# Making the first batch's key and query pieces inside the layer norm, and spreading the expert weight loads over the attention groups

## The reference

```python
x = x + _layernorm(attention(_layernorm(x)))
x = x + _layernorm(moe(_layernorm(x)))

# attention: 16 heads of 16, one key and one value head shared by all
latent = x @ Wc_down                       # 256 -> 128
q = (latent @ Wq_up).reshape(B, T, 16, 16)
k, v = split(latent @ Wkv_up)              # 16 + 16
att = softmax(where(causal, q @ k.T * 0.25, -inf))
y = (att @ v).reshape(B, T, 256) @ Wc_proj

# moe: each token goes to the expert with the largest logit (8 experts, hidden 1024)
y = disp + relu(LN(disp) * g + b @ W1 + b1) @ W2 + b2
```

## Time and profile before

| | us |
|---|---|
| median of 3 runs | 1006.48 |
| profiled execution | 1002.18 |
| its span, first to last instruction | 1000.2 |
| last copy of the latent ends (end of the layer norm) | 38.25 |
| first maxima matmul starts | 54.82 |
| first scores matmul starts | 78.08 |
| busy: PE / PEld / DVE / ACT / POOL | 862.1 / 527.6 / 698.1 / 535.9 / 300.6 |
| mean granted TensorE clock, share of full speed | 0.927 |

### The profile page before, as it was taken

One profiled execution on the slowest core, in us unless ns is written; L12 is line 12 of the kernel. 1 busy time (PEld: TensorE's weight loads), 2 busy tenths in 40 slices (PEclk: granted clock), 3 DMA queues, 4 the chain that ended last, 5 costly groups with the idle time before them and its releaser, 6 DMA issues. The chain is left out here.

```text
span 1000.2 us, 20703 instructions
## 1 busy us (share of the span) xinstructions
PE 862.1 (86%) x5630; PEld 527.6 (53%) x5631; DVE 698.1 (70%) x2447; ACT 535.9 (54%) x909; POOL 300.6 (30%) x565
## 2 busy tenths in 40 slices
PE   5768999999999999999999658851999999999994
PEld 3322333333333333333333147741999999999993
DVE  7457789888888888888886047866466666666652
ACT  3502666666666665666667523311566565656561
POOL 1201223332233322333322123313134344343311
PEclk9955999999999999999999977955999999999998
DMA  9330011111111111211000157732011001011000
GB/s 338 117 103 9 9 52 53 53 42 33 52 64 42 47 35 45 67 45 51 24 25 18 39 200 221 223 127 74 15 31 34 31 31 35 25 33 32 17 16 7
DMA packets 54739, 62.88 MB, mean 63 GB/s; under 512 B 12526, under 2 KB 45958, under 8 KB 54544
## 3 DMA queue, kind: packets, MB, share of 16 engines
q1 hardware_dynamic: 50928, 53.67, 16.1%
q0 software_dynamic: 3744, 8.40, 2.6%
HBM read 35.86 MB, written 9.55 MB: 45 GB/s over the span
## 5 line engine op out<-in xcount | busy, mean ns | idle before, releaser
L592 ACT ACTIVATE PR<-ST 128x1024 f32<-128x1024 f32 (+1 forms) x256 | 239.0, 969 | 150.0 <-PE ST L516 148.4
L645 DVE CUSTOM_DVE_ANT_0 junk<-ring,causal 128x384 bf16<-128x384 f32 (+3 forms) x512 | 220.4, 485 | 35.2 <-PE ring L485 35.0
L485 PE MATMUL ring<-K,Q 96*128 96x512 bf16 (+3 forms) x768 | 208.7, 342 | 41.1 <-DVE MP L645 11.1
L648 DVE TENSOR_REDUCE MP<-ring 128x1 f32<-128x512 f32 x256 | 163.2, 680 | 44.5 <-PE ring L485 44.4
L516 PE MATMUL ST<-Q,K 99*128 99x512 bf16 (+3 forms) x768 | 179.6, 330 | 10.3 <-DMA Q<-MT 6.9
L759 POOL TENSOR_SCALAR_AFFINE_SELECT PR<-PR 128x512 f32<-128x512 f32 x96 | 60.9, 634 | 303.1 <-ACT PR L592 297.8
L1436 PEld LDWEIGHTS hp<-XNT,WS 128*128 128x128 f32 x1248 | 147.8, 195 | 4.9 <-DVE XNT L1508 3.0
L1436 PE MATMUL hp<-XNT,WS 128*128 128x128 f32 x1248 | 148.4, 278 | 2.3 <-DVE XNT L1508 2.3
L485 PEld LDWEIGHTS ring<-K,Q 96*128 96x128 bf16 x768 | 65.8, 99 | 158.2 <-DVE MP L645 59.6
L1444 PE MATMUL yp<-W2s,HT 128*128 x624 | 141.2, 379 | 0.7 <-DVE z L1520 0.7
L533 PE MATMUL OB<-PR,V 128*32 128x512 f32 (+2 forms) x1152 | 124.3, 534 | 0.2
(11 more groups left out here) (173 smaller groups left out, 903.0 us busy)
## 6 DMA issues: line engine op xcount, KB each, us to landing
Q<-T SPq DMA_DIRECT2D x192, 64.0 KB, 2.6
W1s<-in_L_ffn_W_dram SPq DMA_DIRECT2D x8, 1024.0 KB, 12.1
W2s<-in_L_ffn_W_dram SPq DMA_DIRECT2D x8, 1024.0 KB, 7.3
Y<-in_L_attn_x_dram SPq DMA_DIRECT2D x8, 512.0 KB, 6.7
Y<-W1s SPq DMA_DIRECT2D x32, 128.0 KB
XQ<-in_L_attn_x_dram SPq DMA_DIRECT2D x8, 512.0 KB, 3.8
x_rows<-XQ SPq DMA_DIRECT2D x8, 512.0 KB, 7.3
W1s<-den_rows SPq DMA_DIRECT2D x15, 256.0 KB
```

Source lines behind the costliest of these rows:

```text
L485: last = pe.matmul(bank[:, at:at + w], Q[0:NR, g, i // BW, h, i % BW * P:(i % BW + 1) * P], K[b % 2][0:NR, k * NQ:k * NQ + w], start=True, ...
L592: act.activation(PR[t % RB][:, heads[0]:heads[-1] + 1, off:NQ], unit_of(ST[(NU * n + u) % 2], s), ACT.Exp, scale=SCALE).then_inc(exp_done, 1)
L645: op = dve.tensor_tensor_reduce(junk[:, done % 2, at:at + w], src, causal[:, NQ - w:NQ], 1.0, LOWEST, ALU.add, ALU.max, dst)
L648: op = dve.tensor_reduce(dst, src, AX, ALU.max)
```

## The change

It does these things.

1. The six pieces of the first batch move into the layer norm block, in the order k0, q00, k1, q01, q10, q11, at steps 2, 2, 3, 3, 4 and 5 (`FIRST_AT`). At each of these steps TensorE makes the pieces behind the transposes of the step and the `down` of the step before; ScalarE copies part 1 and part 2 at the end of its step; VectorE subtracts at the end of its step, behind the inverse; GpSimd makes part 3 one step later. Two PSUM banks (`room`) and two remainders (`left`) are used in turn.
2. SP sends the first batch's keys and the queries of groups 0 and 1 (6 and 24 DMAs) inside the layer norm block; the queries of groups 2 and 3 are sent at steps s = 5 and s = 9 of group n = 0, 12 DMAs each, without waits.
3. The six W1 loads leave the layer norm block; one is issued at s = 4 of each of the groups n = 0 to 5.
4. Of the four tiles of a layer norm step, VectorE normalises two and GpSimd two. GpSimd's WqT and its constants for K come after its tiles of step 0, the other constants after those of step 1.
5. The copy of the transposes is one instruction of 1024 columns in place of two of 512. The `alone` increments go from the block.

```diff
-FIRST = ("k0", "k1", "q00", "q01", "q10", "q11")
+FIRST = ("k0", "q00", "k1", "q01", "q10", "q11")
+FIRST_AT = {2: ("k0", "q00"), 3: ("k1", "q01"), 4: ("q10",), 5: ("q11",)}
...
             @block.sync
...
-                for e in range(LATE):
-                    sp.dma_start(W1s[:, :, e * F:(e + 1) * F], w1_v[e]).then_inc(w1_in, 16)
+
+                def made(name, part):
+                    sp.wait_ge((first1, first2, first3)[part], FIRST.index(name) + 1)
+
+                sp.wait_ge(ones_set, 6)
+                send_keys(sp, 0, made)
+                for g in range(2):
+                    send_queries(sp, g, made)
...
             @block.gpsimd
...
+                def third(name):
+                    i, _, rest = spot(name)
+                    pool.wait_ge(first2, i + 1)
+                    pool.tensor_tensor(parts(name)[2], rest, parts(name)[1], ALU.subtract).then_inc(first3, 1)
+
+                for t in range(N1):
+                    pool.wait_ge(rstd, t + 1)
+                    past(pool, xt_ready, t - 1)
+                    for i in range(HT, QT):
+                        normalise(pool, t, i).then_inc(xn_pool, 1)
...
+                    for name in FIRST_AT.get(t - 1, ()):
+                        third(name)
...
             @block.vector
...
+                def remainder(name):
+                    i, bank, rest = spot(name)
+                    dve.wait_ge(first1, i + 1)
+                    past(dve, first3, i - 1)
+                    dve.tensor_tensor(rest, bank, parts(name)[0], ALU.subtract).then_inc(first_left, 1)
...
+                for t in range(N1):
+                    if t + 1 < N1:
+                        statistics(t + 1, (t + 1) % 2)
+                    dve.wait_ge(rstd, t + 1)
+                    past(dve, xt_ready, t - 1)
+                    for i in range(HT):
+                        normalise(dve, t, i).then_inc(xn_dve, 1)
+                    if t + 1 < N1:
+                        inverse(t + 1, (t + 1) % 2)
+                    for name in FIRST_AT.get(t, ()):
+                        remainder(name)
...
             @block.tensor
...
+                for t in range(N1):
                     for i in range(QT):
-                        pe.wait_ge(xn_ready, QT * t + i + 1)
+                        if i < HT:
+                            pe.wait_ge(xn_dve, HT * t + i + 1)
+                        else:
+                            pe.wait_ge(xn_pool, HT * t + i - HT + 1)
...
                     last.then_inc(xt_ready, 1)
-                    if beyond(t, 0):
-                        down(t - 1, 1 - k)
-
-                passes(pe, step)
-                down(N1 - 1, 1)
+                    if t:
+                        down(t - 1, (t - 1) % 2)
+                    for name in FIRST_AT.get(t, ()):
+                        i, bank, _ = spot(name)
+                        if i == 0:
+                            pe.wait_ge(wq_turned, 1)
+                        pe.wait_ge(lt_copied, int(name[-1]) + 1)
+                        past(pe, first_left, i - 1)
+                        piece(pe, 0, name, bank).then_inc(first_ready, 1)
+                down(N1 - 1, (N1 - 1) % 2)
...
             @block.scalar
...
+                for t in range(N1):
+                    if t + 1 < N1:
+                        root(t + 1, (t + 1) % 2)
+                    act.wait_ge(xt_ready, t + 1)
+                    act.activation(XT[t % 2][:, :, :], xtp[t % 2][:, :, :], ACT.Copy).then_inc(xt_copied, 1)
+                    if t:
+                        latent(t - 1, (t - 1) % 2)
+                    for name in FIRST_AT.get(t, ()):
+                        i, bank, _ = spot(name)
+                        act.wait_ge(first_ready, i + 1)
+                        act.activation(parts(name)[0], bank, ACT.Copy).then_inc(first1, 1)
+                    for name in FIRST_AT.get(t, ()):
+                        second(name)
+                latent(N1 - 1, (N1 - 1) % 2)
...
         @block.tensor
...
-            pe.wait_ge(masks_made, 6)
-            pe.wait_ge(wq_turned, 1)
-            for name in FIRST:
-                piece(0, name, first_room(name)[0]).then_inc(first_ready, 1)
-            pe.wait_ge(resid, len(FIRST))
             for k in range(EVENT_AT[0]):
                 event(k)
...
         @block.sync
...
-            send_keys(0)
-            for g in range(NG):
-                send_queries(0, g)
             sends(0, EVENT_AT[0])
             for n in range(NB):
                 b, g = divmod(n, NG)
                 for s in range(len(STEPS)):
+                    if n == 0 and s in (5, 9):
+                        send_queries(sp, 2 if s == 5 else 3, lambda name, part: None)
+                    if s == 4 and n < LATE:
+                        sp.dma_start(W1s[:, :, n * F:(n + 1) * F], w1_v[n]).then_inc(w1_in, 16)
```

More of the change, by code:

```diff
@@ L96, in piece_no, with rows_of @@
 def piece_no(b, name):
-    return b * len(FIRST) + (ORDER if b else FIRST).index(name)
+    return (b - 1) * len(ORDER) + ORDER.index(name)
+def rows_of(name):
+    return HD if name[0] == "k" else P
 LEAD = 38
@@ L224, in attention, with parts, weights, piece @@
         eps_set = sem("eps_set")
+        k_in = sem("k_in")
+        q_in = [sem(f"q_in{g}") for g in range(NG)]
+        def parts(name):
+            c = int(name[-1])
+            if name[0] == "k":
+                return [t[:, c * NQ:(c + 1) * NQ] for t in (K1, K2, K3)]
+            return [t[:, int(name[1]), c * NQ:(c + 1) * NQ] for t in (T1, T2, T3)]
+        def weights(name):
+            if name[0] == "k":
+                return Wkv[:, 0:HD]
+            half = 2 * int(name[1])
+            return WqT[:, half:half + 2, :, :].rearrange("p g d h -> p (g d h)")
+        def piece(pe, b, name, bank):
+            c = int(name[-1])
+            return pe.matmul(bank, weights(name), LT[:, b * T + c * NQ:b * T + (c + 1) * NQ], start=True, stop=True)
+        def send_keys(sp, b, made):
+            for r, part in sorted(enumerate(KPART), key=lambda row: row[1]):
+                made("k1", part)
+                sp.dma_start(K[b % 2][r * HD:(r + 1) * HD, :], (K1, K2, K3)[part][:, :]).then_inc(k_in, 16)
+        def send_queries(sp, g, made):
+            half, quarter = divmod(g, 2)
+            rows = slice(quarter * GH * HD, (quarter + 1) * GH * HD)
+            for r, part in enumerate(QPART):
+                made(f"q{half}1", part)
+                for c in range(QC):
+                    sp.dma_start(Q[r * HD:(r + 1) * HD, g, c, :, :].rearrange("d h q -> d (h q)"),
+                                 (T1, T2, T3)[part][rows, half, c * NQ:(c + 1) * NQ]).then_inc(q_in[g], 16)
         with ExitStack() as c2:
@@ L374, in latent, with second @@
                     act.wait_ge(lt_ready, t + 1)
[L375 to L385, removed]
-                root(0, 0)
-                passes(act, step)
-                latent(N1 - 1, 1)
+                    act.activation(LT[:, t * (QT * P):(t + 1) * (QT * P)], ltp[k][:, :], ACT.Copy).then_inc(lt_copied, 1)
+                def second(name):
+                    i, _, rest = spot(name)
+                    act.wait_ge(first_left, i + 1)
+                    act.activation(parts(name)[1], rest, ACT.Copy).then_inc(first2, 1)
+                root(0, 0)
+                for t in range(N1):
[12 more added lines that the diff above has]
+                latent(N1 - 1, (N1 - 1) % 2)
         PR = [sb(f"PR{k}", [P, GH, NQ]) for k in range(RB - 1)]
@@ L456, in _ @@
         def _(pe):
[L457 to L465, removed]
             def values(b, bank):
@@ L501, in event @@
                 else:
[L502 removed]
+                    last = piece(pe, a, b, bank[0:rows_of(b), :])
                 last.then_inc(ring_ready, 1)
@@ L602, in _, with first_part @@
         def _(dve):
[L603 to L608, removed]
+            def first_part(k, b, name):
                 parts_sent(dve, b, name)
@@ L773, in _, with made @@
         def _(sp):
[L774 to L786, removed]
-                    made(b, f"q{half}1", part)
-                    for c in range(QC):
-                        sp.dma_start(Q[r * HD:(r + 1) * HD, g, c, :, :].rearrange("d h q -> d (h q)"),
-                                     (T1, T2, T3)[part][rows, half, c * NQ:(c + 1) * NQ]).then_inc(q_in[g], 16)
+            def made(b):
+                return lambda name, part: sp.wait_ge((part1, part2, part3)[part], piece_no(b, name) + 1)
             def send_max(r, c):
```

116 lines of the change are left out of this document (42 added, 74 removed).

## The result

The changed kernel takes 1008.59 us (median of 12 runs, 1005.82 to 1013.29), the kernel before in the same session 1005.24 (12 runs, 1001.14 to 1007.67). The ratio is 1.0042, 95% interval 1.0029 to 1.0056: slower by 4.2 us, 2.9 to 5.6 (the two medians lie 3.4 us apart; the ratio is made from all runs). The forecast was +3.5 with 0.58 on slower. The profiled execution takes 1005.82 in place of 1002.18, its span is 1004.1 in place of 1000.2. It is the fastest of the 12 runs of the changed kernel. In it the first scores come 3.6 us later, so nearly all of the difference is there by then.

A forecast was written before the change was run, and what follows sets the result against it. Two waits on SP's issue-bound queue stood at the head of the attention. -16.1 - 6.9 + 18.5 (longer layer norm) + 8.0 (clock) = +3.5 us, so 1006.5 becomes 1010.0 us; range 1001.5 to 1014.0.

The forecast's parts named there:

- 0.58 on slower: Whole kernel: the chance given to the change making it slower, against 0.22 for faster and 0.20 for same.
- maxima one hand-over behind the layer norm: Head of the attention: pieces and first sends leave it, so the maxima start right behind the layer norm, -16.1 us.
- scores no longer wait for SP: First scores: with SP's list empty the m row goes out when MT is written, so scores follow the events, -6.9 us.
- steps 0 and 1: Start of the layer norm: these steps don't move much, transposes of step 2 at about 16.7 in both kernels, 0 us.
- loop, at full clock, from step 2 to the end: Layer norm: engine orders close a loop at steps 2 to 5, 8.45 us a two-piece cycle; layer norm ends 18.5 us later.
- clock: Layer norm: four idle gaps of 3.85 us each lose TensorE's full clock, +8 us, with 0 and 24 as the ends.
- first scores: Attention: first scores start at 81.6 in place of 78.08, the sum of all terms, +3.5 us.
- The 2 us a gap: Layer norm gaps: assumed cost of returning to full clock, nearer to the kernel start's 1.5 us lost; +8 for four gaps.
- GpSimd's tile at 0.6 us: Layer norm: GpSimd's normalisation put between a copy (0.411) and a two-input operation (0.772), so 1.2 us a step.
- The first rival: Layer norm: the clock holds through the 3.85 us gaps, sum -4.5, 1002.0 us; chance 0.2.
- the smaller edits: GpSimd's two tiles 0; single 1024-column copy worth nothing; W1 loads hidden by a lead; deferred query DMAs fit into holes.
- the term it called "added": Layer norm: it gets longer because the orders of four engines close a loop at steps 2 to 5, +18.5 us.

The follow-up runs named there:

- the run with the gaps filled: Changed kernel with three more unused f32 matmuls of 512 columns behind the pieces of steps 2 to 5; 999.55 us, ratio 0.9943 to the kernel before.
- three more profiles with the same loop: Changed kernel with ScalarE's table load early (1008.03 us), with GpSimd's constants early as well (1006.07 us), or with the W1 loads back in the layer norm (1010.54 us).
- the version without the loop: Changed kernel with VectorE's remainders and ScalarE's second parts one step later, GpSimd's third parts two, more buffers; 993.41 us, ratio 0.9876 to the kernel before.
- the run with the sends alone: Kernel before with only the queries of groups 2 and 3 sent at s = 5 and s = 9 of group 0; 998.10 us, ratio 0.992.
- the start and SP mended: No-loop kernel with table load and constants early, group 1's queries sent in the attention block, two tiles on GpSimd; 986.21 us, ratio 0.9806 to the kernel before.
- the last version: The no-loop kernel with start and SP mended and two tiles on GpSimd, third parts moved from GpSimd to VectorE; 985.84 us, ratio 0.9809 to the kernel before.
- the gaps and the start mended: Changed kernel, loop kept, with ScalarE's table load early and GpSimd's constants for K, V and MP ahead of its first tile; 1006.07 us, ratio 1.0004.

## Why the prediction was right

Point by point, in the profiled executions:

| term | forecast | measured |
|---|---|---|
| maxima one hand-over behind the layer norm | -16.1 | 16.57 us from layer norm to maxima before, 0.46 after: -16.1 |
| scores no longer wait for SP | -6.9 | 23.26 us from maxima to scores before, 15.96 after: -7.3; alone -7.1 |
| steps 0 and 1 | 0 | +2.9 (step 2 at 19.55, not 16.68) |
| loop, at full clock, from step 2 to the end | 40.1 long (56.8 - 16.7) | 39.4 long, in the run with the gaps filled |
| clock | +8, bounds 0 and 24 | +6.3; in three more profiles with the same loop +7.4, +8.7, +9.8 |
| first scores | +3.5 | +3.6 |

The loop was read off the order of the instruction lists and the durations of the earlier trace rows, and the links came out within 0.3 us each: 8.47 us against 8.45 forecast with two pieces, idle time 3.69 against 3.85; with one piece 7.23 against 7.55, which is most of the 0.7 between 40.1 and 39.4. The order is shown as the cause by the version without the loop, the clock by the one with the gaps filled.

The clock fell once for each of the four gaps, as the Trainium skill has it ("TensorE: Matmul & The Clock Gate", "Why this matters for your kernels"), though mostly after the gap and not in it. The 2 us a gap, chosen between the start of the kernel and a stretch wholly at half, measured 1.6 in the changed kernel's fastest run and 1.9, 2.2 and 2.5 in the three other profiles.

That first scores agree to 0.1 us is luck. The step "Steps 0 and 1 don't move much" failed, by 2.9 us. Of these, 1.2 are the table load, which moved from 1.05 to 6.68 behind the first statistics (the first transposes start at 10.66 and not at 9.45). Another 0.8 are the last tiles of step 1, for which `down` 0 waits: the prediction put GpSimd's tile at 0.6 us, and it takes 1.22 (both bounds, 0.411 and 0.772, were too low; neither row has two scalars read from memory), and GpSimd's constants for K stand ahead of them. The last 0.9 are `down` 0 itself, 3.31 in place of 2.44, and this is scatter of the clock more than the change: in the run with the sends alone, whose layer norm is that of the kernel before, it took 3.08 and step 2 came at 17.73. Against these 2.9 stood a clock that was 1.7 us cheaper in this execution than forecast, 0.7 from the loop and 0.4 from the sends.

The first rival, the faster one, had the condition wrong, as the clock did not hold, and its sum about right: with the clock held by filled gaps the kernel is 5.7 us faster than the kernel before, against the 4.5 that it was given. Of the smaller edits, neither the place of the W1 loads nor GpSimd's share shows an effect in this kernel. No experiment undoes the single copy of 1024 columns.

What the forecast did not say is that the term it called "added" was not needed. The loop closes where VectorE's list has the remainder ahead of the next statistics. Taking it apart was worth 11.7 us at the first scores and 15 to 17 us by the whole times, and with the start and SP mended the same idea is worth 19 us over the kernel before.

## What to carry to other kernels

When work is moved into a pipelined stage, write down for each engine what stands behind the moved instruction on its own list; here a remainder placed ahead of the next step's statistics made four engines take turns, 8.5 us a step in place of 3.2, and placing it one step later brought the steps to 3.6 to 6.5 us. An idle gap of 3.5 us on TensorE was paid twice here, once as the gap and once as half clock in the work behind it, and such a stage scatters: from step 2 to its end the layer norm took 45.7 to 49.2 us in four profiles with the gaps, and 21.57 us in both profiles with the layer norm of the kernel before. When work is moved to another engine, look again for gaps: in the last version one of 2.03 us had half clock behind it, which cost 1.7 us more. Split a change before judging it: the deferred sends alone were worth 8 us, and the longer layer norm hid them.

## What the runs showed that I had not expected

VectorE's normalisation of 128x256 from SBUF to SBUF takes 0.38 to 0.41 us alone, and mostly so beside one of GpSimd's own normalisations (0.57 and 0.64 at most). It stood still while GpSimd ran a two-input operation or a memset: 1.03 us in the changed kernel beside a memset of K, 2.39 us beside two two-input operations of 1.15 each. For the two-input operations this is shown by taking them away; for the memset it rests on the rows. VectorE's statistics show no such rows. It goes the other way too: in the last version a normalisation on GpSimd took 2.16 us in place of 1.22 beside VectorE's third parts, which have two inputs in SBUF, and 1.22 beside its remainders, which have one in PSUM. The Trainium skill has the first half of it ("GPSIMD Engine Reference", "Key points": GpSimd shares its SBUF interfaces with VectorE, and they contend where VectorE runs in a two-port mode or has two SBUF inputs); the runs agree on the two inputs in SBUF. For VectorE's normalisation, which has one tensor input, no run shows whether it is in a two-port mode, and it contended with only some of GpSimd's operations.

A semaphore increment that looked idle had kept ScalarE's table load early: without it the load of 1.28 us stood behind the first wait for data, at 6.68 and not at 1.06.

In the whole times the scatter of such a stage does not show clearly. The runs spread over 11.1 us with the gaps and the start mended (12 runs), but 5.6 to 8.2 us in the other versions with gaps and 6.5 us in the kernel before (12 runs each), which has none in its layer norm; the versions without the loop spread over 2.1 to 4.0 us, with 5 runs each. Fewer runs spread less, so this does not show that gaps make the whole kernel scatter.
